# Clock-keeping products moved between stages, and the first batch ranked ahead in the last expert feed-forward

## The reference

```python
x = conv_nonlocal(x)                       # batch-normed, residual inside
x = x + conv_3x3_mixed_experts(group_norm(x))
t = to_tokens(x)
t = t + attention_4_heads(layer_norm(t))
t = t + ffn_top_k(layer_norm(t))           # 511 of 1024 tokens, 128 -> 512 -> 128, gelu
t = t + attention_16_heads(layer_norm(t))  # latent causal + 256 selected + window of 64
t = t + ffn_experts(layer_norm(t))         # below
```

```python
logits = x @ gate_w + gate_b               # 4096 tokens, 8 experts
probs = softmax(logits); idx = argmax(probs)
one_hot = one_hot(idx)
pos = (cumsum(one_hot, axis=0) * one_hot).sum(-1) - 1      # the token's place in its expert's queue
kept = pos < 640
buf[idx, pos] = x                          # [8, 640, 128], tokens past 640 dropped
y = relu(buf @ w1 + b1) @ w2 + b2
y_tok = y[idx, min(pos, 639)] * prob * kept
```

## Time and profile before

| what | us |
| --- | --- |
| median of 3 runs | 2766.28 (2761.93 to 2774.25) |
| the profiled execution | 2755.48 |
| its span, first to last instruction | 2751.5 |
| TensorE busy | 2476.1 (90%) |
| VectorE busy | 1885.7 (69%) |
| ScalarE busy | 1462.4 (53%) |
| GpSimd busy | 1309.9 (48%) |
| mean granted TensorE clock | 0.944 |
| DMA moved | 131.61 MB |

### The profile page before, as it was taken

How to read it: one execution, slowest core, us unless ns; L and a number is a source line. 1 busy time by engine, 2 the same in 40 slices (tenths; PEclk the granted TensorE clock), 3 DMA queues, 4 the chain that set the end, 5 groups by cost and what they waited for, 6 DMA issues and landing times. The chain is left out here.

```text
span 2751.5 us, 52837 instructions
## 1 busy us (share of the span) xinstructions
PE 2476.1 (90%) x17187; PEld 1731.3 (63%) x17187; DVE 1885.7 (69%) x3715; ACT 1462.4 (53%) x2524; POOL 1309.9 (48%) x884
## 2 busy tenths in 40 slices
PE   5599996765899999999999999999999999999777
PEld 3466664554566666666666666666666666666766
DVE  2767764667486776877767768677686776877526
ACT  1124553332366657666576665666666657666223
POOL 0213681000245637557375573664746647457235
PEclk8699998877999999999999999999999999999788
DMA  3003310011431121120211202122112121120242
GB/s 113 1 12 87 68 26 9 1 46 58 112 87 43 33 51 35 43 55 15 51 35 43 55 15 51 35 47 51 29 38 44 38 51 35 43 55 15 74 139 69
DMA packets 85079, 131.61 MB, mean 48 GB/s; under 512 B 16224, under 2 KB 60769, under 8 KB 84625
## 3 DMA queue, kind: packets, MB, share of 16 engines
q1 hardware_dynamic: 81328, 123.16, 17.7%
q0 software_dynamic: 3024, 7.43, 0.8%
q10 hardware_dynamic: 656, 0.09, 0.0%
HBM read 63.49 MB, written 20.79 MB: 31 GB/s over the span
## 5 line engine op out<-in xcount | busy, mean ns | idle before, releaser
L2467 ACT ACTIVATE a_PT<-PS 128x512 f32<-128x512 f32 (+1 forms) x1111 | 613.7, 586 | 343.0 <-PE PS L2330 235.5
L2188 POOL TENSOR_TENSOR a_KT<-a_PT 128x512 f32<-128x512 f32 (+2 forms) x179 | 418.5, 2353 | 466.0 <-ACT a_PT L2467 464.0
L2188 POOL TENSOR_TENSOR a_KT<-a_KT,a_PT 128x2048 f32<-128x2048 f32 (+3 forms) x128 | 391.8, 3061 | 8.8
L2536 DVE TENSOR_REDUCE a_NM<-PS 128x2 fp32r<-128x512 f32 x460 | 297.1, 687 | 120.2 <-PE PS L2280 116.5
L2329 PE MATMUL PS<-a_QH,a_KSW 128*128 128x256 f32 (+2 forms) x848 | 305.2, 379 | 7.1 <-ACT a_PT L2467 7.1
L2329 PE MATMUL PS<-a_QH,a_K 128*128 128x512 f32 (+3 forms) x768 | 306.9, 406 | 0.0
L2550 DVE TENSOR_REDUCE a_MX<-PS 128x1 f32<-128x512 f32 (+3 forms) x432 | 267.3, 665 | 39.2 <-PE PS L2291 21.2
L2330 PE MATMUL PS<-a_QL,a_K1B 76*128 76x512 f32 (+3 forms) x768 | 262.1, 348 | 0.0
L2291 PE MATMUL PS<-a_K,a_QH 128*128 128x512 f32 (+3 forms) x768 | 253.2, 397 | 0.0
L2277 PE MATMUL PS<-a_KSW,a_QH 128*128 128x512 f32 x460 | 196.2, 476 | 29.4 <-DVE a_QL L2520 29.4
L2523 DVE TENSOR_TENSOR a_KSW<-PS,a_KSW 64x512 fp32r<-64x512 f32 x170 | 117.2, 690 | 126.6 <-ACT a_KSW L2426 123.4
(11 more groups left out here) (437 smaller groups left out, 5573.1 us busy)
## 6 DMA issues: line engine op xcount, KB each, us to landing
a_KWB<-a_KSW SPq DMA_DIRECT2D x68, 256.0 KB, 3.3
a_K1B<-a_K SPq DMA_DIRECT2D x32, 512.0 KB, 5.3
a_XC<-latents SPq DMA_DIRECT2D x17, 512.0 KB, 3.9
a_CKS<-latents SPq DMA_DIRECT2D x17, 512.0 KB, 4.6
a_CF<-latents SPq DMA_DIRECT2D x17, 448.0 KB, 4.1
slots<-in_empty_slots SPq DMA_DIRECT2D x1, 5160.0 KB, 18.7
f_XB<-slots SPq DMA_DIRECT2D x8, 645.0 KB, 8.9
c_EX<-in_experts SPq DMA_DIRECT2D x1, 4608.0 KB, 17.3
```

What stands on the lines that cost most here:

```text
L2188: nc.gpsimd.tensor_tensor(total, one_in, other_in, ALU.add).then_inc(s["added"], 1)
L2467: nc.scalar.activation(PT[:, to:to + width], turning(key)[:, 0:width], ACT.Exp).then_inc(s["taken"], 1)
L2536: ins = nc.vector.tensor_reduce(out, bank.rearrange("p (a n) -> p a n", a=2), AX.X, ALU.max, negate=True)
```

## The change

Five things are changed. The holds in stage_ffn2 (30) and stage_latents (45) are gone. In stage_heads, near_scores for block 0, head 0 issues nine of keep_clock's products into its own bank, between the wait for the bank and the wait for the splits; the scores' first product then overwrites them. In stage_ffn3 the first part of the statistics covers batch 0 alone (8 tiles) and the second the other 24; batch 0 is normalised, turned, and placed ahead of the rest, with VectorE's, ScalarE's and TensorE's orders rewritten for it; TensorE's first hold is 16 products and waits for nothing, and the second is 80 products, ahead of the wait for the slots and in another bank. SP loads the rows of experts 0, 1 and 2 one by one, each after the one before has landed, and those of the others behind their predecessor's weights.

```diff
@@ stage_ffn2
-                hold_clock(nc, P[7], ident, 30)
                 scores(0)
@@ stage_latents
-                hold_clock(nc, P[7], ident, 45)
                 norm_tensor(nc, pe, s, 0, P, XNs[0], ident)
@@ stage_heads, near_scores
-                    after(pe, q, at, bank_free(key, q), *(("reduced", ("split", "tr", g)) for g in made))
                     bank, k0, w = ring(key), max(0, i - 1) * 128, 256 if i else 128
+                    after(pe, q, at, bank_free(key, q))
+                    if i == 0 and h == 0:
+                        keep_clock(9, bank)
+                    after(pe, q, at, *(("reduced", ("split", "tr", g)) for g in made))
@@ stage_heads, keep_clock
-                def keep_clock(count):
+                def keep_clock(count, bank=P[7]):
 
                     for _ in range(count):
-                        nc.tensor.matmul(P[7][:, 0:384], identb[:, :], masks.rearrange("p a n -> p (a n)"), start=True, stop=True)
+                        nc.tensor.matmul(bank[:, 0:384], identb[:, :], masks.rearrange("p a n -> p (a n)"), start=True, stop=True)
@@ stage_ffn3, SP
-                for e in range(E3):
+                def load_tokens(e):
                     sp.dma_start(XB[:, e, :, :], slots[e * CAP:(e + 1) * CAP, :].rearrange("(t p) c -> p t c", p=128))\
                         .then_inc(x_ld[e], 16)
+
+                for e in range(3):
+                    load_tokens(e)
+                    sp.wait_ge(x_ld[e], 16)
                 for e in range(2, E3):
                     load_weights(e)
+                    if e + 1 < E3:
+                        load_tokens(e + 1)
@@ stage_ffn3, TensorE
+                hold_clock(nc, P[7], ident, 16)
+                turn_batch(0)
                 pe.wait_ge(s["ld"], 96)
                 pe.wait_ge(s["one"], 1)
-                hold_clock(nc, P[7], ident, 45)
-                for b in range(B):
-                    turn_batch(b)
-                    if b == B - 1:
-                        ranks(0)
-                    logits(b)
-                for b in range(1, B):
-                    ranks(b)
+                logits(0)
+                turn_batch(1)
+                ranks(0)
+                logits(1)
+                turn_batch(2)
+                logits(2)
+                turn_batch(3)
+                ranks(1)
+                logits(3)
+                ranks(2)
+                ranks(3)
+                hold_clock(nc, P[4], ident, 80)
                 pe.wait_ge(s["slot_ready"], B)
-                hold_clock(nc, P[7], ident, 90)
                 turn_tokens(0)
@@ stage_ffn3, ScalarE (root, keep_beside and keep_turned are the loops of before cut into functions)
+                root(0)
+                keep_beside(0)
+                keep_turned(0)
+                root(1)
+                exponentials(0)
+                keep_turned(1)
+                keep_beside(1)
+                keep_turned(2)
+                exponentials(1)
+                keep_turned(3)
+                exponentials(2)
+                keep_beside(2)
+                exponentials(3)
+                keep_beside(3)
                 keep_tokens(0)
@@ stage_ffn3, VectorE
+        part = lambda h: slice(h * NT, TT if h else NT)
...
+                moments(0).then_inc(s["stat"], 1)
                 statistics(0)
+                moments(1)
+                normalise(0)
+                moments(2)
+                moments(3).then_inc(s["stat"], 1)
                 statistics(1)
-                normalise(0)
-                normalise(1)
                 dve.wait_ge(s["ld"], 96)
                 nc.vector.tensor_copy(XA[:, :, IDS].bitcast(U32), row_of[:, :])
+                shift(0)
+                normalise(1)
+                choose(0)
                 normalise(2)
-                shift(0)
+                place(0)
+                shift(1)
                 normalise(3)
-                choose(0)
-                shift(1)
-                place(0)
                 choose(1)
```

More of the change, by code:

```diff
@@ L1346, in exponentials, with root, keep_beside, keep_turned @@
                     nc.scalar.activation(A1[:, of(b), :], LG[:, of(b), :], ACT.Exp).then_inc(s["exp"], 1)
-                for h in range(2):
+                def root(h):
                     act.wait_ge(s["var"], h + 1)
[L1350 to L1354, removed]
+                    nc.scalar.activation(deviation[:, part(h)], va[:, part(h)], ACT.Sqrt).then_inc(s["std"], 1)
+                def keep_beside(b):
+                    nc.scalar.activation(XA[:, of(b), C:2 * C], T[:, of(b), :], ACT.Copy).then_inc(s["beside"], 1)
+                def keep_turned(b):
                     for h in range(2):
@@ L1380, in _, with moments @@
                 link = Chain(dve, s["sub"])
+                def moments(b):
+                    for t in range(b * NT, (b + 1) * NT):
+                        ins = nc.vector.bn_stats(st[:, t, :], T[:, t, :])
+                    return ins
                 def statistics(h):
[L1384 to L1387, removed]
+                    half = part(h)
                     dve.wait_ge(s["stat"], h * 3 + 1)
@@ L1400, in normalise @@
                 def normalise(b):
-                    if b % 2 == 0:
-                        half = slice(b * NT, (b + 2) * NT)
-                        dve.wait_ge(s["std"], b // 2 + 1)
-                        nc.vector.reciprocal(inverse[:, half], deviation[:, half]).then_inc(s["inv"], 1)
-                        dve.wait_ge(s["inv"], b // 2 + 1)
+                    if b < 2:
+                        dve.wait_ge(s["std"], b + 1)
+                        nc.vector.reciprocal(inverse[:, part(b)], deviation[:, part(b)]).then_inc(s["inv"], 1)
+                        dve.wait_ge(s["inv"], b + 1)
                     for t in range(b * NT, (b + 1) * NT):
```

## The result

The changed kernel takes 2800.34 us (median of 4 runs, 2785.45 to 2806.34) against 2764.11 for before in the same runs: the ratio is 1.0128, 95% interval 1.0098 to 1.0159. It is slower, by more than the forecast of 2781.1 and beyond the range of 2765 to 2795.

A forecast was written before the change was run, and what follows sets the result against it. It took TensorE to bound the head loop, about 1,800 of 2,751.5 us. Terms +23.8 + 0.5 (prologue) + 8 - 4 + 1.5 - 15 = +14.8 on the median 2766.28 gave 2781.1; range 2765 to 2795.

The forecast's parts named there:

- The nine products, +23.8: Head loop, near_scores for block 0, head 0: products hidden by no wait, 1.49 us a pass, 23.8 in 16 passes.
- The clock in the loop, +8: Head loop: longer passes move the 1.64 us wait, so some 8 more passes fall at 1.3 us each; taken as +8.
- The bound of 18 for this term: Head loop: upper bound on the cost of further clock falls, 14 x 1.3 = 18 us.
- The latents, -4: Latents without their hold: transposes start some 8 us earlier but on a half clock; net -4 us (bounds -8 and -1).
- The top-k feed-forward, +1.5: Second feed-forward without its hold: earlier start, but cold work and cold hidden products behind; +1.5 us (bounds -3 and +4).
- The expert feed-forward, -15: Last feed-forward: the new order brings tokens at +74.9 instead of +96.9; 15 us gained after deductions (bounds -22 and -7).
- GpSimd's gap: Last feed-forward: a gap of 2.81 us on POOL that no row explains, deducted from the gain as 2.8.
- The cold first expert: Last feed-forward: the hold of 80 ends 3 to 7 us before the tokens, so a half-clock start costs about 2.
- The 11.2 us ahead of place(3): Last feed-forward in before: a wait without known cause; 2 us deducted for a short wait of that kind.
- Rival (b): Last feed-forward: the unexplained 11.2 us come before place(1), so only 7 is gained; +22.8, 2789 us; chance 0.15.
- Rival (a): Head loop: fewer falls, moved passes keep the clock, and the feed-forward gains 19; +2.8, 2769 us; chance 0.18.
- Rival (c): Head loop: the products fill a wait and hold the clock, costing 0 and saving 2.6; -20, 2746 us; chance 0.07.

The follow-up runs named there:

- e7: The changed kernel with nine products at both places, also in the wait ahead of near_scores(4, 0): 2757.58 us, ratio 1.0007 to before.
- e3: The changed kernel with its nine products moved into the recurring wait ahead of near_scores(4, 0), in the eighth bank: 2728.50 us, ratio 0.9918 to before.
- e1: The kernel before with only the nine products at near_scores(0, 0) added: 2805.78 us, ratio 1.0175 to before.
- e4: The changed kernel with 21 products in place of nine, at the same place: 2793.74 us, ratio 1.0140 to before.
- e12: The changed kernel with 64 unread products instead of 60 ahead of the head loop's prologue: 2783.12 us, ratio 1.0108 to before.
- e13: The changed kernel with 76 unread products instead of 60 ahead of the head loop's prologue: 2781.57 us in one execution.

## Why the prediction was wrong, step by step

- **The nine products, +23.8: right.** That both waits of near_scores(0, 0) are one event, that TensorE does not wait there and pays in full, was read off the diff and the earlier trace rows. A pass without a fall went from 112.60 to 114.08 us, and e7 measures 23.7 for all of them, the prologue's nine included.
- **The clock in the loop, +8: the step that failed, by its size.** The step has a mechanism and two numbers. The mechanism stood up: the wait is where the clock falls (e3, e7: filled, it never does), and a pass of another length falls another number of times (e1, e4). That it is the place of the wait in time that decides is inferred from this, and from one and the same loop falling 2 to 8 times; no row shows what makes a place good. The numbers were too small. How often: eight falls more than before's two were forecast (10.4 us, taken at 8); 11 and 12 more came in the changed kernel, 13 more in e1, e12 and e13. What each costs: 1.3 us was the mean of before's two, both short (1.6 and 0.9 over the pass of 112.6). Double falls were not in that sample. In e1, e12 and e13 every second one is double: 115.02 - 114.08 = 0.94 for a short and 117.06 - 114.08 = 2.98 for a double one. In e1 the eight short and seven double falls take 28.3 us, 25.7 more than before's 2.6, in place of 8; with the products' 23.7 that is the 49.4 by which its heads are longer.
- **Waits without a named cause, not foreseen: +13.8.** This is the term that the sum lacked, and in the changed kernel it is larger than the excess of the falls. From 832.84 to 2575.94 its 15 full passes take 31.9 us more than 15 x 114.08. The three waits of 4.59, 4.45 and 4.71 are 13.8 of that, and 18.1 are left for 13 falls: 16.6 for the ten in other passes, and 0.5 each for the three in the passes with such a wait, where the slow clock runs in the wait for a_QL. Less the 2.6 of before, the clock's term is 15.5 where 8 was forecast: 23.7 + 15.5 + 13.8 = 53.0, for 52.9 measured. Nothing in before's head loop pointed to these waits. Without them the heads are as long (e12), because more passes fall, and more of them double; so the falls alone suffice for the 53 us, and their size is the step that had to be right.
- The Trainium skill, TensorE: Matmul & The Clock Gate, section on the HAM's oscillation, tells of a kernel that waits some 3 to 5 us for a DMA in every turn of its loop, and whose clock falls back in every turn. The waits here, 1.64 to 1.73 us, are about half as long or less, so the prediction's reading, all 16 passes, went beyond the page. The runs come out that way at this pass length (15 of 15 in three kernels), and not at others: 2 in before and 5 in e4, with a wait as long.
- **The bound of 18 for this term** was 14 further falls at 1.3 us each. In the changed kernel the term measured 15.5, inside the bound, but with 13.8 of unnamed waits beside it, for which the range had no room. Without such waits it measured 25.7 in e1 and 28.5 in e12, outside the bound. A price taken from two samples needed a bound of its own.
- **The latents, -4: right** (-3.9). Their transposes started 8.3 us earlier in the stage and took 2.05 us for eight:

```profile
570.60 2.05 PE L460 MATMUL PS<-ident,l_XN 128*128 128x128 f32 x8 [17.36 <-DVE l_XN L440]
```

- **The top-k feed-forward, +1.5: wrong in sign**, -2.3, inside its bounds (over all traces 120.3 us in the mean without the hold, 121.6 with it; the latents 124.9 and 128.3). The clock was back before the hidden products: the two products of the scores ran cold, the eight transposes behind them took 1.10 us, as with the hold (1.09).

```profile
451.04 3.78 PE L1058 MATMUL PS<-f_XC,f_wrr 128*128 128x512 f32 x4 [0.69 <-ACT f_XC L452]
...
455.60 1.10 PE L966 MATMUL PS<-ident,f_rk_row 128*128 128x128 f32 x8 [0.78 <-ACT f_rk_row L1094]
```

- **The expert feed-forward, -15: close** (-13.7), for partly other reasons. The chain up to the last scatter was right to 2.6 us at every point (+21.1, +35.9, +68.5 for +22.7, +38.5, +68.8), and so was GpSimd's gap (2.64 for 2.81). The forecast of tokens at +74.9 holds in all seven kernels whose hold of 80 runs without gaps (+74.2 to +74.5); in the changed kernel the hold ended last instead. The cold first expert, taken at 2, costs 2 to 4. The 11.2 us ahead of place(3) did not come back in full in any of the ten traces of the new order. In the two of the changed kernel a shorter wait of that kind did: place(3) at +54.3 and +55.9, where the other eight have +49.4. It is hidden behind the scatters of batch 2 in the first, and GpSimd waits 1.92 us for it in the second. Rival (b), the wait ahead of place(1), did not happen. The serial loads of the tokens stayed hidden: the four whose landing the trace has took 4.1 to 5.6 us.
- **Rival (a)**, fewer falls, was off in the direction: the passes fell more often, not less. Its mark of seven falls was also loosely set: at 1.3 each, 13.8 us are reached with five more falls if the feed-forward gains 15, and with eight or nine if it gains 19. **Rival (c)**, products that fill a wait, is what e3 does at the other place, and there its price was right: 2.6 us of falls saved and nothing paid.
- **The time itself.** The steps gave 2755.5 + 14.8 = 2770.3. The falls add 15.5 - 8 = 7.5, the unnamed waits 13.8, the expert feed-forward 1.3; the top-k feed-forward takes 3.8 off, and the two stages in front, never part of the change, add 10.7 in this trace: 2799.8 beside the measured 2799.88 (the products came 0.6 under their 24.3, and 0.7 more lay around the span). So 10.7 us of the distance in this execution belong to no step of the prediction.

## What to carry to other kernels

Before putting unread products into a wait, look in the timeline whether the engine waits at that very instruction, and whether the wait ahead of them and the wait behind them are for different events; at the right place nine products cost nothing here and kept the clock, 40 us ahead of it they cost 24 us and left a clock that fell in nearly every pass. In a loop whose wait can let the clock fall, a change of the pass's length is a change of the clock as well: price both kinds of fall, or fill the wait first and then change the length. And compare stages, not only whole times: what was not changed moved by up to 19 us between traces.

## What was not expected of the hardware

- A loop settles. With the same wait of 1.64 us in each pass, before's loop fell 2, 5, 7 or 8 times in its first passes and then never again in any of six traces; so does the loop of 116.03 us (5, then none). A loop of 114.08 us never does: 13 to 15 of 15. Each fall makes its pass longer and so moves the next wait. Why a loop settles at one length and not at another is not shown here.
- Falls come short and double (0.91 and 0.83 in a window of 20 us). A short one cost 0.9 or 1.6 us of the pass, a double one mostly 2.5 to 3.0.
- A fall can cost almost nothing: 0.5 us where the slow clock ran into the wait for a_QL and filled it.
- Four products more or less in a program of 17,000 on TensorE decide over 26 packets of instructions and waits of 4.5 to 4.8 us at three places, over gaps in a run of identical products (+83 and +79 against +74 for the tokens), and over 11 us on VectorE. Nothing in the diff foretold it; only a second kernel with shifted code showed it.
